# A vision and text transformer block on one core: the second normalisation's statistics taken in the attention stage, and the second quantisation taken from ScalarE to VectorE

## What is computed

```
h = concat(patch_embedding(x), text_embedding(x_txt))          # (64, 228, 192)
h = h + attention(layernorm(h))
h = h + ffn(layernorm(h))

def bitlinear(x, w, g):
    xn = x * rsqrt(mean(x * x) + 1e-6) * g                      # over the last axis
    scale = 127 / max(max(abs(xn)), 1e-5)
    return (round(xn * scale) / scale) @ ternary(w).T
ffn(x) = bitlinear(gelu(bitlinear(x, w1, g1)), w2, g2)          # 192 -> 768 -> 192
```

## Time and profile before

| what | value |
|---|---|
| median of 3 runs | 1919.89 us (1918.67 to 1920.64) |
| the profiled execution, its own time | 1918.11 us |
| its span in the profile | 1916.4 us |
| mean granted clock of TensorE | 0.882 of full |
| busy share of the span: PE, PEld, DVE, ACT, POOL | 84%, 71%, 72%, 61%, 57% |
| set-up, attention stage, FFN stage | about 0 to 100, 100 to 1389, 1389 to 1916 us |

### The profile page before, as it was taken

The page is one execution under the profiler, slowest core; times in us unless marked ns, Lnnn a source line. Parts: engine busy times, 40 slices in busy tenths (PEclk is TensorE's granted clock), DMA queues, the critical chain, the costliest instruction groups (busy, mean ns, idle before and its releaser), DMA issues.

```text
span 1916.4 us, 50514 instructions
## 1 busy us (share of the span) xinstructions
PE 1614.7 (84%) x16574; PEld 1363.0 (71%) x16574; DVE 1371.2 (72%) x3151; ACT 1171.3 (61%) x1830; POOL 1089.9 (57%) x1503
## 2 busy tenths in 40 slices
PE   0539999999999999999999999999556666666666
PEld 0438888888888888888888888887445555555555
DVE  3635666666666666666666666666289999999996
ACT  1124555555555555555555555555278888888887
POOL 5035555555555555555555555554177777777775
PEclk9969999999999999999999999999666666666665
DMA  8564656565656565656565656561000000000000
GB/s 103 137 116 69 100 78 99 79 100 78 100 79 100 78 99 80 100 79 99 80 100 78 99 80 100 79 99 26 24 12 22 22 22 22 22 22 22 22 22 26
DMA packets 159967, 132.96 MB, mean 69 GB/s; under 512 B 32558, under 2 KB 151040, under 8 KB 159808
## 3 DMA queue, kind: packets, MB, share of 16 engines
q1 hardware_dynamic: 159168, 131.00, 44.0%
q0 software_dynamic: 768, 1.57, 0.5%
HBM read 118.32 MB, written 11.91 MB: 68 GB/s over the span
## 4 chain that ended last, share of the span: by engine, by line
PE 70%; DVE 14%; issue 5%; SPq 4%; ACT 3%; DMA 2%; POOL 1%; DVEq 1%; ACTq 0%; POOLq 0%
PE ps L1072 24%; PE ps L1154 8%; PE ps L1237 7%; PE ps L1228 7%; DVE ff_st L857 4%; PE ps L1184 4%; PE ps L1216 3%; PE ps L1189 3%; PE ps L1210 3%; PE ps L1314 3%; PE ps L1333 2%; DVE xpix L838 2%; PE ps L1145 2%; PE ps L1135 1%; PE ps L1168 1%
## 5 line engine op out<-in xcount | busy, mean ns | idle before, releaser
L1072 PE MATMUL ps<-w_eff,xpix 118*112 118x193 f32 (+1 forms) x2048 | 457.2, 362 | 21.0 <-POOL side L438 20.4
L1072 PEld LDWEIGHTS ps<-w_eff,xpix 118*112 118x112 f32 (+1 forms) x2048 | 387.8, 253 | 39.8 <-issue 32.8
L915 ACT ACTIVATE probs<-ps,isw 116x688 f32<-116x688 f32 x384 | 298.7, 830 | 175.6 <-PE ps L1216 175.6
L449 POOL TENSOR_TENSOR xsq<-xsq 118x784 f32<-118x784 f32 (+2 forms) x192 | 221.8, 1155 | 293.6 <-ACT xsq L909 283.5
L738 DVE TENSOR_REDUCE nmax<-ps 116x12 bf16<-116x1344 f32 (+2 forms) x192 | 302.2, 1574 | 108.7 <-PE ps L1189 103.8
L524 POOL TENSOR_TENSOR xpix<-probs,g_b 112x192 f32<-112x192 f32 (+1 forms) x512 | 296.5, 609 | 109.0 <-ACT probs L1024 99.7
L469 POOL TENSOR_SCALAR_AFFINE_SELECT probs<-probs 116x464 f32<-116x464 f32 x384 | 268.4, 717 | 46.5 <-ACT probs L915 31.0
L682 DVE TENSOR_SCALAR front_st<-ps 112x1 f32<-112x1 f32 (+1 forms) x128 | 18.3, 152 | 229.2 <-PE ps L1135 218.1
L1314 PE MATMUL ps<-w1t,xpix 96*112 96x384 f16 (+1 forms) x512 | 160.7, 488 | 14.5 <-ACT xpix L1015 13.3
L1154 PE MATMUL ps<-xnT,wq_pad 97*128 97x228 f32 (+1 forms) x768 | 166.0, 365 | 0.0
L1303 PE MATMUL ps<-ident_h,xpix 112*96 112x112 f16 (+1 forms) x256 | 34.9, 281 | 152.9 <-DVE xpix L874 152.9
(11 more groups left out here) (160 smaller groups left out, 3393.3 us busy)
## 6 DMA issues: line engine op xcount, KB each, us to landing
xpix<-in_x SPq DMA_DIRECT2D x192, 196.0 KB
xpix<-in_x SPq DMA_DIRECT2D x192, 195.1 KB
rden<-den_rows SPq DMA_DIRECT2D x256, 85.5 KB, 2.2
out<-xpix SPq DMA_DIRECT2D x64, 87.0 KB
out<-xpix SPq DMA_DIRECT2D x64, 84.0 KB
xpix<-in_x SPq DMA_DIRECT2D x128, 34.1 KB
xpix<-in_x SPq DMA_DIRECT2D x128, 34.0 KB
den<-o_sb SPq DMA_DIRECT2D x256, 2.7 KB
```

What stands on the lines that cost most here:

```text
L449: nc.gpsimd.tensor_tensor(out_, a, b, ALU.add).then_inc(s_ssq, 1)
L915: A(probs[0:TB, g, 2 * e:2 * e + 2, :], ps[0:TB, 4 + 2 * e:6 + 2 * e, 0:SK], ACT.Exp, scale=isw[0:TB, 7:8]).then_inc(s_p, 1)
L1072: last = MM(ps_tok[tile][0:P, :], src, w_eff[0:HI, o, :], start=(o == 0), stop=(o == OFFS - 1))
```

## The change

In the attention stage DVE gets a new last part of each step, `measure(n-1)`: mean and variance of the second normalisation for the image whose attention was just added, and the first maxima. POOL gets `row_roots(n-2)`, one power per image, between `patch_roots` and `clear_later(n,0)`. Behind the stage five small DVE instructions make the first scales of all images at once. In the FFN stage DVE no longer does that work and quantises image i-1 itself (`quantise_second`); ACT no longer does (`quantise` is gone). The root of the GELU's squares stays on POOL, but as `gelu_roots(n)` behind the weighting of the same image, with the addition of the epsilon on POOL too; the division by 768 goes into the scale of ACT's square. `f_q2` becomes one semaphore for each tile, and PE turns the first tile without waiting for the second. `v1` gets a buffer of its own.

```diff
+            def row_roots(m):
+                pool.wait_ge(s_var2, m + 1)
+                nc.gpsimd.tensor_tensor(rms[:, bass.ds(m * 2, 2)], ln_st[:, 32:34], expo[:, 0:2],
+                                        ALU.pow).then_inc(s_rms, 1)
...
                 if newer:
                     patch_roots(n + 2)
+                if prev:
+                    row_roots(n - 2)
                 if old:
                     clear_later(n, 0)
...
+            def weight(n, b):
+                after(pool, f_q2[0], n - 1)
+                after(pool, f_q2[1], n - 1)
+                for tile, P in enumerate((TA, TB)):
+                    pool.wait_ge(f_g, 2 * n + tile + 1)
+                    for lo in range(0, HIDDEN, HIDDEN // 4):
...
+            def gelu_roots(n, b):
+                pool.wait_ge(f_ssq, 2 * n + 2)
+                apart(pool)
+                nc.gpsimd.tensor_scalar(ff_st[:, b, 18:20], gel_sum[:, b, :], EPS_RMS, None,
+                                        ALU.add).then_inc(f_var, 1)
+                pool.wait_ge(f_var, n + 1)
+                nc.gpsimd.tensor_tensor(ff_st[:, b, 20:22], ff_st[:, b, 18:20], expo[:, 0:2],
+                                        ALU.pow).then_inc(f_r1, 1)
...
+            def measure(n):
...
+                dve.wait_ge(s_h2, n + 1)
+                apart(dve)
+                for tile, P in enumerate((TA, TB)):
+                    last = V.bn_stats(ln_st[0:P, 20 + 6 * tile:26 + 6 * tile], h_all[0:P, hcols(n, tile)])
+                chain(last, 1)
+                apart(dve)
+                for tile, P in enumerate((TA, TB)):
+                    last = V.bn_aggr(ln_st[0:P, 34 + 2 * tile:36 + 2 * tile], ln_st[0:P, 20 + 6 * tile:26 + 6 * tile])
+                chain(last, 2)
+                after(dve, s_rms, n)
+                V.tensor_scalar(ln_st[:, 32:34], ln_st[:, 35:38:2], 1.0 + EPS_RMS,
+                                EPS_LN * EPS_RMS, ALU.mult, ALU.add).then_inc(s_var2, 1)
+                V.tensor_copy(mean2[:, bass.ds(n * 2, 2)], ln_st[:, 34:38:2])
+                for tile, P in enumerate((TA, TB)):
+                    last = V.scalar_tensor_tensor(v1[0:P, tile, :], h_all[0:P, hcols(n, tile)],
+                                                  ln_st[0:P, 34 + 2 * tile:35 + 2 * tile], g1_b[0:P, :],
+                                                  ALU.subtract, ALU.mult)
+                chain(last, 3)
+                for tile, P in enumerate((TA, TB)):
+                    last = V.tensor_reduce(peak[0:P, bass.ds(n * 2 + tile, 1)], v1[0:P, tile, :], AX_X, ALU.max,
+                                           apply_absolute_value=True)
+                last.then_inc(s_peak, 1)
...
                 if new:
                     maxima(n + 1, 2)
+                if prev:
+                    measure(n - 1)
...
+            def ffn_step(i, b, new=True, mid=True, last_=True):
+
+                if new:
+                    centre(i + 1)
+                if last_:
+                    final(i - 3, 1 - b)
                 if mid:
...
+                    peaks(i - 1, 1 - b)
+                if new:
+                    quantise_first(i + 1)
                 if mid:
...
+                    second_scales(i - 1, 1 - b)
+                    quantise_second(i - 1, 1 - b)
...
+            def quantise_second(n, b):
+                dve.wait_ge(f_sc, n + 1)
+                after(dve, f_t2, n)
+                for tile, P in enumerate((TA, TB)):
+                    V.tensor_scalar(q2[0:P, tile, :], v2[0:P, b, tile, :], ff_st[0:P, b, 38 + tile:39 + tile],
+                                    MAGIC16, ALU.mult, ALU.add).then_inc(f_q2[tile], 1)
...
-                if mid:
-                    quantise(i, b, 0)
-                    quantise(i, b, 1)
```

More of the change, by code:

```diff
@@ L238, in build @@
         f_v2 = sem("gelu_weighted")
-        f_q2 = sem("second_quantised")
+        f_q2 = [sem(f"second_quantised{i}") for i in range(2)]
         f_t2 = sem("second_transposed")
@@ L529, in _ @@
-            ffn_step(-1, 1, mid=False)
-            ffn_step(0, 0, mid=False)
-            ffn_step(1, 1)
-            ffn_step(2, 0)
-            ffn_step(3, 1)
-            with pool.Fori(2, PAIRS - 1) as t:
+            row_roots(IMAGES - 2)
+            row_roots(IMAGES - 1)
+            def weight(n, b):
[4 more added lines that the diff above has]
+                    for lo in range(0, HIDDEN, HIDDEN // 4):
+                        cols = slice(lo, lo + HIDDEN // 4)
+                        last = nc.gpsimd.tensor_tensor(v2[0:P, b, tile, cols], gel[0:P, b, tile, cols],
+                                                       g2_b[0:P, cols], ALU.mult)
+                    last.then_inc(f_v2, 1)
@@ new lines, in gelu_roots @@
+            def gelu_roots(n, b):
[6 more added lines that the diff above has]
+                                        ALU.pow).then_inc(f_r1, 1)
+            weight(0, 0)
@@ L535, in _ @@
+            gelu_roots(0, 0)
+            weight(1, 1)
+            gelu_roots(1, 1)
+            with pool.Fori(1, PAIRS) as t:
                 for b in range(2):
-                    ffn_step(2 * t + b, b)
-            ffn_step(IMAGES - 2, 0)
-            ffn_step(IMAGES - 1, 1, new=False)
-            ffn_step(IMAGES, 0, new=False)
+                    weight(2 * t + b, b)
+                    gelu_roots(2 * t + b, b)
         @block.vector
@@ L566, in _ @@
             step(V.memset(nmax[:, :, :], 0.0))
+            for filled in (mean2, rms, peak):
+                step(V.memset(filled[:, :], 1.0))
             dve.wait_ge(s_const, 32)
@@ L888, in _ @@
             ffn_step(IMAGES - 1, 1, new=False)
-            ffn_step(IMAGES, 0, new=False, skipped=3)
+            ffn_step(IMAGES, 0, new=False)
             ffn_step(IMAGES + 1, 1, new=False, mid=False)
```

180 lines of the change are left out of this document (79 added, 101 removed).

## The result

| what | before | changed |
|---|---|---|
| median, us | 1919.53 (1918.67 to 1920.64) | 1948.69 (1945.79 to 1950.78) |
| span of the profiled execution | 1916.4 | 1947.2 |
| ratio to before | | 1.0151 (95% interval 1.0133 to 1.0168) |
| attention step, `front` to `front` | 19.18 to 19.20 | 19.57 |
| FFN step (spacing of `final`, mean of 52 steps) | 7.97 | 8.09 |

The change costs 29 us; 1910 was forecast, with a range up to 1942. The stages share the loss: the last `add` starts at 1388.28 before and at 1407.92 now, 19.6 us later, and from its end to the end of the span it is 11.2 us more. The attention stage loses half of what was forecast (39). The FFN stage, which should have gained 47, gains nothing. The error is there.

What follows compares the result with a forecast made beforehand. PE was taken to bound the attention stage and DVE to be nearest to bounding the FFN stage. From 1918.1 us, +39 (attention), -47 (FFN), +1 and -1 (edges) gave 1910 us, range 1882 to 1942.

Steps and rivals of the forecast that it cites:

- `measure` at nothing: Attention stage, DVE: `measure` takes 2.7 us, fits the 3.40 us gap before `front`, and costs nothing.
- The power at PE, 0.65 per image, +39 us: Attention stage: POOL's new power delays its clearings, so PE waits 0.65 us per image; 60 x 0.65 = +39 us.
- the low bound of 0.3: Attention stage: the power uses 0.53 us in which POOL stood still behind `aT`, leaving a shift of about 0.3 us.
- The second rival: Attention stage: the power is half hidden behind `aT`, PE waits only 0.3 us per image; total 1889 us; chance 0.20.
- The sum of DVE's FFN step, 7.1: FFN stage: DVE's remaining and added instructions sum to 7.1 us per step; step taken at 7.15 against 7.93, -47 us.
- the pair L882: FFN stage, DVE: the first quantisation's two instructions keep their earlier busy time of 0.80 us per step.
- The small arithmetic: FFN stage, DVE: the small scale instructions up to the quantisation take 1.35 us per step.
- the high bound, 7.9: FFN stage: a whole POOL piece before each second quantisation, 2 x (0.55 + 0.6), makes the step 7.9 us, no gain.
- The round of ACT and PE, 6.6 to 7.6: FFN stage: ACT's GELU and PE's product wait on each other in a round of 6.6 to 7.6 us per step.
- The third rival: FFN stage: the ACT and TensorE round becomes the bound, step stays at 7.6; slower, total 1937 us; chance 0.23.
- The fourth rival, ports held: Shared SBUF ports are held for whole instructions: attention +50 us, FFN step 7.5 for -26; total 1942 us; chance 0.15.
- Edges: Between the stages, small instructions, `centre` and a quantisation replace the old first step, +1 us; set-up 0; final drain -1.

Runs made afterwards that it cites:

- Experiment 1: The changed kernel with POOL's new power row_roots put ahead of patch_roots; 1926.9 us, 1.0044 of the kernel before.
- experiment 4: The changed kernel with POOL's wait for its own first tile's pieces put back between the two tiles; 1899.6 us, 0.9883 of the kernel before.
- experiment 6: The changed kernel with row_roots ahead of patch_roots and POOL's wait between the tiles put back; 1877.3 us, 0.9778 of the kernel before.
- experiment 12: The changed kernel with one POOL wait on itself per image, behind the sixth piece of eight; 1922.9 us, 1.0024 of the kernel before.

## Why the prediction was wrong

By its own steps.

*`measure` at nothing*: right. It took 3.1 us of the 3.40 and `front` still waits for PE.

*The power at PE, 0.65 per image, +39 us*: right in mechanism (PE's L1273 waits for POOL's L486 and nothing else), wrong in size. It was 0.38, some 20 us with the loop's edges, within the bounds of 18 to 50 that were kept. The term that failed is the shift. The prediction saw that the power would be held by `aT` and the clearing no longer; it wrote the low bound of 0.3 down from just that, and then took 0.65. The second rival's price for this stage was the right one. Experiment 1 shows the wait to be the whole of it.

*The sum of DVE's FFN step, 7.1*: this is the step that failed. Of its terms the maxima (1.77 forecast, 1.88), `centre` (0.86, 0.91), `final` (0.74, 0.81) came out near. The quantisation pair L919 was put at 1.5 and took 1.31. But the pair L882, put at 0.80, took 1.87: this is the term that broke the sum, and with POOL's wait back it takes 0.91. The small arithmetic, from L907 to L919, was put at 1.35 and took 1.80 on average; 1.53 of that is there with the wait too. Its 1.35 was read from one step, while the mean of the same stretch before is 1.51. DVE's idle time of 0.29 ahead of L882, for its own maxima, was in no term. The row for L882 came from a kernel in which DVE waits for at most one piece of POOL. Even the high bound, 7.9, was worked out as "a whole POOL piece before each". That property was a result of one wait in POOL's program, which the change takes out, and the prediction costed that removal at nothing: it doesn't name it. With the wait the same step is 7.30 (experiment 4) against 7.15 forecast, and 1899.6 would have been 10 us below the forecast, mostly for the smaller attention term. The addition on POOL, which no row showed and which was put at 0.5 to 0.7, takes 0.22 where nothing holds it; POOL was not the bound, so this changed nothing.

*The round of ACT and PE, 6.6 to 7.6*: it did not bind. ACT is idle before its GELU, for PE's L1359, for 132.9 of 460 us where it was 42.1, and with the second quantisation on it again ACT reaches 6.83. The third rival's sign came true, its mechanism did not: the step would have had to stay at 7.6 for want of PE, and it went to 8.09 for want of DVE.

*The fourth rival, ports held*: nearest in time (1942), but by luck: it had +50 for the attention stage, where some 20 were measured, and -26 for the FFN steps, where 60 x (8.09 - 7.97) = +7 were. It was partly right about who fights whom. The row first: L767 starts at 701.50, while the power L466 is running (701.02, 0.70 us), and takes 0.86 us, no more than L746 of as many columns (one input from PSUM) with no power beside it. In the FFN stage 72 of the quantisations L919 start while a power (L546) is running, and they take 600 to 622 ns, where this line's shortest is 600 and its mean 655. So a running power holds none of these up; a running piece of 192 columns does, as L882 shows, and a running `aT` holds the next power (1.24 for 0.70). The Trainium skill, SBUF — State Buffer, Who interferes with whom, calls the pair of ports that VectorE and GpSimd share "an exclusive lock". For the pieces the trace agrees; for a running power it does not, and the measurement stands. But by that rule alone a DVE instruction that asks during a piece waits for the rest of that piece, 0.55 us at the most, and the prediction's high bound was priced so (the rival itself priced only POOL being held); the 2.6 us of the longest instance (L882 from 1467.05 on) are five pieces that began while DVE was already waiting. The forecast of POOL being held by the two long quantisations is seen too (the power L546 takes 1.23 on average in place of 0.70), and costs nothing as long as POOL is not the bound.

*Edges*: from the end of the last `add` to the first quantisation it is 1414.31 - 1408.54 = 5.8 us, before 1392.76 - 1388.90 = 3.9. Forecast +1, measured +1.9.

## What to carry to other kernels

A wait of an engine on itself that guards no data can still do work: here it broke up a run of GpSimd instructions behind which VectorE's stood. When a change takes such a wait out, or makes a run of GpSimd instructions longer, look for single VectorE instances far above the shortest, since means and busy shares hide them, and compare the longest with the longest of before. Where many short GpSimd instructions stand in a row beside VectorE work, try one such wait every few of them: here one in eight, in the middle, was worth 49 to 118 us, and one in two cost 9 us more than that one.

## What was not expected of the hardware

- GpSimd's tensor_tensor pieces that follow each other without a break can keep a waiting VectorE instruction out for several pieces: 2.64 us for 128 x 4 elements, while pieces of 0.55 us ran. For the first quantisation the excess over its shortest was at most 0.42 us with four in a row (0.46 in experiment 6), 1.43 with six, 2.62 with eight. Not every request is kept out. In the changed kernel the 42 long ones begin during the second to fifth piece of the eight and none during the last three; in experiment 12 the 37 begin during the second or third of the six, again none during the last three. With four in a row, a request during the second or third piece is one during the last three, and none is kept out. So that one wait helps requests ahead of it fits; why the last three pieces differ stays open, and so does why some requests during the second to fifth piece are not kept out either.
- A wait that is already fulfilled does not break a run: the wait for `f_g` stands between the tiles in all the kernels here. The one that helped makes POOL wait for its own last result, 0.21 us. Whether any other pause of that length would do as well was not tried.
- VectorE's maxima over 768 columns are not held by the same pieces: 934 to 945 ns beside them in the changed kernel.
- A second power put where POOL stood still anyway cost 0.38 us of its 0.70, and ahead of the wait, nothing.
